# Attention and sandwich layer on one core: the maxima's score matmuls begin by twos, with none behind the weighing in odd steps

## The reference, cut to what matters

```
energy = einsum('nqhd,nkhd->nqkh', q, k)
att = softmax(energy / scale, axis=2)
out = einsum('nqkh,nkhd->nqhd', att, v)
```

## Time and profile before

| what | value |
|---|---|
| median of three runs | 3422.21 us (3420.38 to 3422.49) |
| span of the profiled execution | 3418.2 us |
| its own time | not listed apart from its span; the median lies 4.0 us above the span |
| PE busy | 3280.1 us, 96% of the span |
| DVE busy | 2961.0 us, 87% |
| ACT busy | 2896.0 us, 85% |
| POOL busy | 976.6 us, 29% |
| granted TensorE clock | 0.986 of full speed, mean |

### The profile page before, as it was taken

How to read it: one execution, slowest core, us unless ns; L and a number is a source line. 1 busy time by engine, 2 the same in 40 slices (tenths; PEclk the granted TensorE clock), 3 DMA queues, 4 the chain that set the end, 5 groups by cost and what they waited for, 6 DMA issues and landing times.

```text
span 3418.2 us, 55797 instructions
## 1 busy us (share of the span) xinstructions
PE 3280.1 (96%) x19328; PEld 931.1 (27%) x19328; DVE 2961.0 (87%) x5517; ACT 2896.0 (85%) x3806; POOL 976.6 (29%) x1382
## 2 busy tenths in 40 slices
PE   6989999999999999999999999999999999999987
PEld 2222232322323232232322323232232322323222
DVE  7999989888898988989888898988989888898942
ACT  3868979798897979889798897979989798896975
POOL 5012060421506033060421406033060421505024
PEclk7998999999999999999999999999999999999999
DMA  3111111121112111111121111111121121111001
GB/s 89 26 41 43 37 44 32 43 49 43 51 33 54 39 49 43 43 50 32 43 50 43 51 33 50 41 46 47 36 57 33 43 49 44 38 32 50 7 22 37
DMA packets 97337, 144.71 MB, mean 42 GB/s; under 512 B 49312, under 2 KB 59936, under 8 KB 89248
## 3 DMA queue, kind: packets, MB, share of 16 engines
q1 hardware_dynamic: 93360, 123.83, 13.7%
q0 software_dynamic: 3696, 17.31, 2.7%
HBM read 34.61 MB, written 32.51 MB: 20 GB/s over the span
## 4 chain that ended last, share of the span: by engine, by line
PE 69%; DVE 14%; ACT 8%; issue 4%; SPq 2%; POOL 2%; DMA 1%; DVEq 0%; POOLq 0%
PE heads_ps L503 24%; PE ring_ps L470 15%; PE scoresT_ps L488 11%; DVE max_parts L949 10%; PE scoresT_ps L590 7%; ACT p_sb L700 4%; PE scoresT_ps L595 3%; DVE stats L960 2%; PE scoresT_ps L598 2%; ACT headsT L709 1%; PE scoresT_ps L601 1%; PE ring_ps L532 1%; SPq L337 1%; PE scoresT_ps L518 1%; PE heads_ps L470 1%
## 5 line engine op out<-in xcount | busy, mean ns | idle before, releaser
L949 DVE TENSOR_REDUCE max_parts<-ring_ps 128x1 f32<-128x512 f32 x3741 | 2365.5, 682 | 230.0 <-PE ring_ps L470 171.1
L700 ACT ACTIVATE p_sb<-scoresT_ps 128x1024 f32<-128x1024 f32 x2048 | 1970.2, 1025 | 84.6 <-PE scoresT_ps L488 60.8
L470 PE MATMUL ring_ps<-k_rows,q_rows 48*128 48x512 bf16 x3741 | 1078.0, 385 | 23.5 <-DVE max_parts L949 14.4
L503 PE MATMUL heads_ps<-p_sb,v_sb 128*9 128x512 f32 x8192 | 1073.3, 596 | 17.9 <-ACT headsT L709 11.9
L488 PE MATMUL scoresT_ps<-q_rows,k_rows 51*128 51x512 bf16 x4096 | 1021.8, 384 | 15.0 <-ACT p_sb L700 7.5
L470 PEld LDWEIGHTS ring_ps<-k_rows,q_rows 48*128 48x128 bf16 x3741 | 263.5, 94 | 1319.9 <-DVE max_parts L949 1209.6
L1210 POOL CAST max_wide<-max_all 128x16 bf16<-128x16 f32 x128 | 25.1, 196 | 1753.7 <-DVE max_all L955 1753.7
L590 PE MATMUL scoresT_ps<-state,w 128*128 128x512 f32 x736 | 365.4, 619 | 5.9 <-DVE state L1013 3.9
L488 PEld LDWEIGHTS scoresT_ps<-q_rows,k_rows 51*128 51x128 bf16 x4096 | 207.7, 94 | 243.7 <-ACT p_sb L700 219.9
L811 ACT ACTIVATE p_sb<-scoresT_ps,b 128x512 f32<-128x512 f32 x180 | 123.5, 686 | 165.6 <-PE scoresT_ps L590 164.6
L503 PEld LDWEIGHTS heads_ps<-p_sb,v_sb 128*9 128x9 f32 x8192 | 124.7, 89 | 289.6 <-issue 278.6
(11 more groups left out here) (206 smaller groups left out, 2757.7 us busy)
## 6 DMA issues: line engine op xcount, KB each, us to landing
q_rows<-parts SPq DMA_DIRECT2D x744, 32.0 KB
k_rows<-parts SPq DMA_DIRECT2D x744, 32.0 KB
x_sb<-in_x SPq DMA_DIRECT2D x16, 1024.0 KB, 4.9
x_in<-in_x SPq DMA_DIRECT2D x15, 1024.0 KB, 5.1
out<-x_sb SPq DMA_DIRECT2D x15, 1024.0 KB, 3.9
out<-x_in POOLq DMA_DIRECT2D x15, 1024.0 KB, 7.8
q_rows<-max_rows SPq DMA_DIRECT2D x512, 3.0 KB
feat_h<-headsT SPq DMA_DIRECT2D x512, 16.0 KB
```

What stands on the lines that cost most here:

```text
L470: e.matmul(ring_bank(max_taken, u + 1), q_rows[rows, slot, pair, h * BANK + qb * P:h * BANK + (qb + 1) * P], k_rows[rows, slot, pair, kh * ...
L503: m = e.matmul(heads_ps[32 * j:32 * j + DH + 1, :], v_sb[:, b % 2, kb, 4 * (group % NG) + j, 0:DH + 1], p_sb[:, n % 2, j, :], start=(kb == ...
L700: e.activation(p_sb[:, n % 2, 2 * two:2 * two + 2, :].rearrange("p h n -> p (h n)"), scoresT_ps[:, 2 * two * BANK:(2 * two + 2) * BANK], A ...
L949: e.tensor_reduce(max_parts[:, gi % 2, kh, col:col + 1], bank_of(max_taken, u + 1), AX.X, ALU.max).then_inc(max_taken, 1)
```

## The change

It replaces the table of batches 1 to 15. Before, every step had two units behind the first scores, none behind the second and one behind the weighing. Now every step has two behind the first scores; an even step has two behind the weighing and an odd step none. A pair of steps still has six units, and each group of two begins with an even unit, one of side 0.

```diff
@@ -222,7 +222,7 @@
                 return 0
             if b == 0:
                 return units_until(LEAD0 + 4 * n + (1, 3, 4)[third])
-            return units_until(b * UNITS + LEAD + min(IN_ATTENTION, 3 * n + (2, 2, 3)[third]))
+            return units_until(b * UNITS + LEAD + min(IN_ATTENTION, 6 * (n // 2) + ((2, 2, 4), (6, 6, 6))[n % 2][third]))
 
         def units_in_beat(b, j):
             if b == -1:
```

## The result

The changed kernel takes 3597.86 us (median of four runs, 3595.72 to 3605.08); the kernel before, beside it, 3421.30 us. The ratio is 1.0519, with a 95% interval of 1.0504 to 1.0534: slower by 176.6 us. Forecast were 3597 us, within 3573 to 3625.

What follows compares the result with a forecast made beforehand. It took a 3.97 us loop through ScalarE and TensorE as the bound, replaced by 4.42 us through VectorE and TensorE. 167 us (batches 1 to 14) plus 8.7 (batch 15), together 176, gave 3598, taken as 3597; range 3573 to 3625.

Steps and rivals of the forecast that it cites:

- The loop of before: Old pair of steps: 3.97 us through ScalarE's exponential, weighing, lone unit and scores on TensorE; VectorE not in it.
- Part one: Odd step's lone unit gone from behind its weighing: at most 0.22 us to TensorE, nothing by the loop.
- part two: Even step ends with two units, sides 0 and 1, sharing one slot: nothing gained or lost.
- Part three, D's wait: Fourth unit D behind the even step's weighing needs first unit A's bank: 0.73 us wait, pair 4.42 us.
- The eviction hidden: Eviction of `heads_ps` every eight steps, 0.30 us on ScalarE, hidden by 0.24 us of room and earlier exponentials.
- The sum: Batches 1 to 14: 167 us more; batch 15: 8.7; batch 0, beats and ending untouched; together 176.
- The clock's rival: TensorE's idle gaps lower its granted clock at times, 1.6 us each; one a batch makes 3620 us; 5%.
- VectorE's idle time ahead of L949: Before the maxima on VectorE, batches 1 to 14: idle time grows by some 0.5 us a pair.
- Faster by pairing: Six units and eight scores take seven slots instead of eight; at best 14 us less, 3408 us; 3%.
- TensorEngine Tiling (Array Packing): Tiles' matmuls in parallel, taken alone: up to one slot a pair, 104 us less; counted within the faster rival's 3%.
- the pressure on PSUM: Skill page's Gotcha 1: row tiling increases pressure on PSUM; taken to decide over parallel tiles.
- No change, by throughput: Waiting D only uses time TensorE would have waited for ScalarE, six maxima taking 3.69 us; 3422 us; 3%.

Runs made afterwards that it cites:

- e4: Kernel before the change with the maxima (L949) taken over 256 of 512 columns; 3381.62 us, ratio 0.9882.
- e6: Kernel before with table (2, 3, 3) and (5, 6, 6), each step's lone unit behind the second scores, ahead of the weighing; 3427.39 us, ratio 1.0018.
- e1: Kernel before with table (2, 2, 3) and (6, 6, 6): four units between even weighing and odd second scores, not paired by sides; 3596.02 us, ratio 1.0509.
- e5: Changed kernel with the maxima taken over 64 of 512 columns; 3378.75 us, ratio 0.9878 to the kernel before.
- e3: Changed kernel with the maxima (L949) taken over 256 of 512 columns; 3451.64 us, ratio 1.0086 to the kernel before.

## Why the prediction was right

- **The loop of before** (3.97 us through the even step's lone unit): that VectorE is not in it is shown by e4, in which the pair did not move when VectorE's work was cut by 0.265 us a maximum. That ScalarE closes it is argued from rows, and e6, which moved the unit and kept the pair, fits. No run shortened an exponential, and TensorE's own queue is nearly as long as the loop: it is busy for 127.97 of 129.90 us, and the even step's second scores come 0.72 us behind its first, the odd step's 0.62, so the wait for ScalarE is worth some 0.1 us a pair.
- **Part one and part two, the pairing** (nothing gained or lost): e1 has no pairing and the same 4.42 us and 3596 us.
- **Part three, D's wait** (1.17 us behind A instead of 0.44): 1202.55 - 1201.38 = 1.17. The counted places hold too: weighing 1.71 behind A (1203.09), the next first scores 2.69 (1204.07). ScalarE's second exponential of the odd step begins 1.81 behind A, at 1203.19, as counted.
- **The eviction hidden**: an attention has grown by 11.7 to 11.8 us, as the forecast's 11.9 with the eviction won back has it; 31 pairs of 0.46 without it would be 14.3. Two evictions in a row of batch 4's attention show it directly. They begin 17.67 us apart, four pairs of 4.42 and nothing more:

```profile
1011.88 0.60 ACT L709 ACTIVATE headsT<-heads_ps 128x512 f32<-128x512 f32 x1
1029.55 0.60 ACT L709 ACTIVATE headsT<-heads_ps 128x512 f32<-128x512 f32 x1
```

- **The sum**: 14 x 11.7 = 164 where the forecast had 167, and batch 15's 48 steps 8.8 where it had 8.7 (106.2 against 97.4, once 1.6 for a fall of the clock is taken off the 107.80 of this profile). Together 173 of the 176.6 measured between the medians. The loop was right; that the total came within 1 us is partly luck, for the forecast's 3 us too many in the attentions stand against falls of the clock, which its sum put at nothing. The clock's rival came true in a small part beside the forecast: in the profiled execution, the longest of the four at 3605.08 us, five attentions of batches 1 to 14 hold a short fall of the clock against two before, 1.6 us each (batch 1's lasts twice as long), and the ending has a mean of 0.89 and takes 140.20 us against 134.4:

```profile
3323.80:3431.60 107.80, 99.08 (x714) 18.55 (x713) 91.77 (x150) 97.94 (x106) 9.09 (x21) 0.98 0.03 6
3463.00:3603.20 140.20, 114.18 (x296) 45.95 (x296) 52.89 (x141) 68.23 (x115) 61.39 (x58) 0.89 0.15 35
```

- **One sign was mis-sized**: VectorE's idle time ahead of L949 was to grow by some 0.5 us a pair. In batch 4's attention it is 19.9 us against 8.8 before, over 32 pairs 0.35 us. The attention as a whole grew by no more than 0.37 us a pair (11.7 over 32), since the evictions' time was won back; that share of the 0.46 never became idle time. Nothing in the sum hung on it.
- **The rivals.** "Faster by pairing" needed A's bank to be free 0.44 us behind A, and it was free at 1.17; in e5, at 0.71, nothing is gained either. In TensorEngine Tiling (Array Packing) of the Trainium skill, Key Properties, tiles run in parallel, and the trace agrees (A and B share one row at 1201.38), but the gain has no place in the loop that sets the time: e1, with the units unpaired, has the same 4.42 us. Of the pressure on PSUM, which the prediction let decide, the runs show the narrower form: four units in a row on three banks cost the same whether they are paired or not. "No change, by throughput" fell with the result itself: six maxima at 0.615 us would fit into 3.69 us, and the pair took 4.42.

## What to carry to other kernels

With R buffers in a ring and an engine that issues in order, unit k+R must not be wanted before unit k's buffer is released: measure how far apart they begin (here 1.17 us from a matmul to the reuse of its bank when the consumer is free at once) and spread units to that distance, whatever the mean rate. A burst of R+1 puts the consumer's latency into the producer's queue, and everything behind it. The consumer may be idle for much of the time and still be on the path; to see it, shorten its work alone in both orders, as e3 and e4 do. No run here had a fourth bank, so what more buffers would give back is not shown.

## What was not expected of the hardware

The maximum over PSUM took 683, 418 and 220 ns for 512, 256 and 64 columns: about 1.03 ns a column and some 150 ns fixed. Short falls of the granted clock to half of full speed came in two attentions of batches 1 to 14 before and in five after, one profile each. The order does not account for them: e4 has three, and e6, with the old pair of steps, four; e3, in the changed order, has none. Their cause is open.
